# Layer 1 attention, first steps: the eighth tile's score matmuls moved to steps 0 and 1, and three other moves

## The chip, the cores and the metric

The kernel runs as one program on 1 core of one Trainium2 chip. The metric is the device time of one execution in microseconds (us); lower is better. Engines are named as the profile names them: PE (TensorE matmuls) and PEld (its weight loads), DVE (VectorE), ACT (ScalarE), POOL (GpSimd), SP (SyncE, which starts the plain DMAs). Each engine works its own list of instructions in order and waits on semaphores that the others raise.

## The reference, cut to what matters

Two layers on 4 x 1024 rows of 256 numbers. Layer 0 is a causal cross attention and a mixture of eight experts. The change lies where layer 0's experts end and layer 1's attention begins:

```
x = x + L0_ffn(layernorm(x))                    # top-2 of 8 experts per row
# layer 1: 16 heads of width 16 over 77 keys, no mask
q = layernorm(x) as (rows, 16 heads, 16), then @ Wq
energy = q . k ;  attention = softmax(energy / 16)
x = x + (attention @ v) @ Wo.T + bo
x = x + L1_ffn(layernorm(x))                    # gelu, low rank
```

## The kernel before, in words

`experts_and_attend` writes out one list per engine by hand. The first part of each list is the expert part: 32 full steps of 256 row slots (`step(t)`), each with an up and a down product, whose results ACT copies out (`y`) and SP stores to DRAM. The last ones run together with the preparation of layer 1's first row tiles. The second part is a loop over `k in STEPS` (0 to 32).

Layer 1 works on 32 tiles of 128 rows, `f` = 0 to 31. To make a tile ready takes:

1. `gather(f)` on POOL: two indirect DMAs fetch the rows' two expert results. The first 8 tiles use stores that are done earlier; from `f == 8` on `gather` waits for the last store of the expert part.
2. `rows_in_full(f)` on DVE: weigh and add them, then mean and variance (last instruction: `ve_a`, L2001).
3. `deviation(f)` on POOL: the power -1/2 (L1415) and the shift (L1418).
4. `normed_rows(f)` on ACT (L1848), `rows_transposed(f)` on PE (L1713), `high(f)` on ACT (L1842) and `low(f)` on DVE: the normalised rows, transposed, as two float16 parts.
5. `scores(f, i)` on PE (L1644), i = 0 to 3, each followed by `maximum(f, i)` on DVE (L2010): the energies of a tile, a quarter at a time, of which only the row maximum is kept. All quarters of the later tiles share one PSUM bank, so quarter i + 1 waits for the maximum of quarter i. `maxima(g)` and `maxima_transposed(g)` then prepare the maxima of four tiles.

Eight tiles (`AHEAD`, `SOON_ROWS = 8`) go through 1 to 4 during the expert part, and seven of them (`EARLY`) through 5. The eighth tile (number 7) has its scores in step k = 2.

A group of four tiles (512 rows) has four steps, one for four heads each. Step k does `scores_by_key(k)` on PE (L1673, energies with keys on partitions, ending with a fourth term that subtracts the maxima), two `exps(k, half)` on ACT (L1854, softmax's exponentials), and, for the step before, `values(k-1)` on PE (L1685) and `values_out(k-1)` on ACT (L1860). Beside it, it takes tile f = k + 5 through 5, tile k + 6 through 4 and tile k + 7 through 2. From k = 5 on it also finishes tile k - 5 (heads, projection, residual). PE's step begins with `scores(k + 5, 0)`, which waits for `high(k + 5)`. In steps 0 to 4 PE also runs `awake(4)` up to three times (L1719): products into an unused bank whose result nobody reads.

On ACT a step is `normed_rows(f + 1)`, `exps(k, 0)`, (heads,) `values_out(k - 1)`, `exps(k, 1)`, `high(f + 1)`. On POOL an iteration for tile f is `gather(f + 2)`, `deviation(f)`, `biased(f - 8)` (L1424). The exponentials need another function table on ACT than the experts' gelu. L1819, behind the last copy of `y`, runs one exponential of a 128 x 1 tile (`early_a`), so that the table is loaded there.

Of the kernel before, what the change touches and what calls it, by code (L numbers as in the profile page):

```python
# [31 lines left out]
P = 128  # L32
# [1254 lines left out]
def experts_and_attend(nc, A, G):  # L1287
# [3 lines left out]
    with ExitStack() as ctx:  # L1291
# [38 lines left out]
        rec = Q.sb("rec_a", [P, 2, HEADS])  # L1330
        o = Q.sb("o_a", [P, 2, D])
        oT = Q.sb("oT_a", [P, 2, D])
        early = Q.sb("early_a", [P, 1])
        banks = ctx.enter_context(nc.psum_tensor("banks_ea", [P, 8, 512], F32))
        up_ps, xT_ps, y_ps = [banks[:, i, :] for i in range(4)], banks[:, 4, :], [banks[:, i, :] for i in (5, 6)]
        sT_ps, pr_bank, v_ps, s_ps, t_bank = banks[:, 0:4, :], banks[:, 4, :], banks[:, 5, :], banks[:, 6, :], banks[:, 7, :]
# [34 lines left out]
        with nc.Block() as block:  # L1371

            @block.gpsimd
            def _(pool):
# [72 lines left out]
                pool.wait_ge(k1_ok, KN)  # L1447
                pool.wait_ge(bo_in, 16)
                for f in range(SOON_ROWS, NT):
                    if f + 2 < NT:  # L1450
                        gather(f + 2)
                    deviation(f)
                    if f >= LAG:
                        biased(f - LAG)
                for f in range(NT - LAG, NT):
# [38 lines left out]
            def _(pe):  # L1494
# [161 lines left out]
                def scores_by_key(k):  # L1656
                    g, c, i = k // 4, k % 4 // 2, k % 2
                    b, slot = g // 2, g % 3
                    pe.wait_ge(lo_ok, 4 * g + 4)
                    after(pe, exp_ok, 2 * k)  # L1660
                    for term in range(4):
                        if term == 3:
                            pe.wait_ge(mT_ok, g + 1)
                            if tile(k + 5) and k + 5 not in EARLY:
                                scores(k + 5, 1)
                        for r in range(4):
                            rows, head = slice(32 * r, 32 * r + 32), 8 * c + 2 * r + i
                            keys = ds(head * KEYS, KEYS)
                            w, v = ((G["khi"][1][rows, b, keys], xhi[slot][rows, c, :]),
                                    (G["khi"][1][rows, b, keys], xlo[slot][rows, c, :]),  # L1670
                                    (G["klo1"][rows, b, keys], xhi[slot][rows, c, :]),
                                    (mrows[rows, 2 * c + i, :], mT[rows, g % 2, :]))[term]
                            last = mm(sT_ps[0:KEYS, r, :], w, v, start=term == 0, stop=term == 3)  # L1673
                            if term == 3 and r % 2:
                                last.then_inc(sT_done, 1)
# [40 lines left out]
                def awake(count):  # L1716

                    for i in range(count):
                        mm(pr_ps, G["ident16"][:, :], G["khi"][1][:, 0, 0:D], start=True, stop=True)  # L1719
# [18 lines left out]
                for k in STEPS:  # L1738
                    f, n = k + 5, k - 5
                    filled = 0 <= k < 5  # L1740
                    if tile(n):
                        heads_out(n, k)
                    late = tile(f) and f not in EARLY
                    if late:
                        scores(f, 0)
                    if 0 <= k < QUARTERS:
                        scores_by_key(k)
                    if filled:
                        if k == 4:
                            pe.wait_ge(mT_ok, 2)  # L1750
                        awake(4)
                    if tile(n):
                        heads_transposed(n)
                    if 0 <= k - 1 < QUARTERS:
                        values(k - 1)
                    if late:
                        scores(f, 2)
                    if filled:
                        awake(4)
                    if tile(n):  # L1760
                        projection(n)
                    if tile(f + 1) and f + 1 not in AHEAD:
                        rows_transposed(f + 1)
                    if filled:
                        awake(4)
                    if late:
                        scores(f, 3)
                    if (k + 1) % 4 == 0 and 0 <= (k + 1) // 4 < GROUPS:
                        maxima_transposed((k + 1) // 4)
# [11 lines left out]
            def _(act):  # L1781
# [11 lines left out]
                def step(t):  # L1793
                    for q in range(QS):
                        act.wait_ge(up_done, FIRST_Q + QS * t + q + 1)
                        if isinstance(t, int) and t == 0 and q < 2:
                            act.wait_ge(turned, 2 * (SH - 1) + q + 1)
                        else:
                            act.wait_ge(hlo_ok, FIRST_Q + QS * t + q - 1)
                        nc.scalar.activation(h[:, q % 2, :], up_ps[q], ACT.Gelu, scale=1 / WSCALE).then_inc(gelu_ok, 1)  # L1800
                        if isinstance(t, int) and t == 0 and q == 1:
                            short_result(SH - 1)
                    f = t - TURNED if isinstance(t, int) else -1
                    if f in AHEAD:
                        normed_rows(f)
                    if not isinstance(t, int) or t + 1 < FULL:
                        rows(SH + t + 1)
                    if f in AHEAD:
                        high(f)
                    if isinstance(t, int) and t + 1 == FULL:  # L1810
                        maxima(0)
                    act.wait_ge(down_done, FIRST_DOWN + QS * t + QS)
                    act.wait_ge(y_out, stored(t))
                    if isinstance(t, int) and t == 0:
                        act.wait_ge(odd_out, 16 * (SH // 2))
                    for n in range(2):
                        nc.scalar.activation(y[:, n, :], y_ps[n][:, 0:D], ACT.Copy, scale=1 / WSCALE).then_inc(y_ok, 1)  # L1817
                    if isinstance(t, int) and t + 1 == FULL:
                        nc.scalar.activation(early[:, :], G["neghalf"][:, :], ACT.Exp)  # L1819

                def short_result(s):
                    act.wait_ge(down_done, s + 1)
# [62 lines left out]
                for k in STEPS:  # L1885
                    f, n = k + 5, k - 5
                    ahead = not tile(f + 1) or f + 1 in AHEAD
                    if not ahead:
                        normed_rows(f + 1)
                    if 0 <= k < QUARTERS:  # L1890
                        exps(k, 0)
                    if tile(n):
                        heads(n)
                    if 0 <= k - 1 < QUARTERS:
                        values_out(k - 1)
                    if 0 <= k < QUARTERS:
                        exps(k, 1)
                    if not ahead:
                        high(f + 1)
                    if (k + 1) % 4 == 0 and 0 <= (k + 1) // 4 < GROUPS:  # L1900
                        maxima((k + 1) // 4)
# [8 lines left out]
            def _(dve):  # L1910
# [156 lines left out]
                for k in STEPS:  # L2067
# [2 lines left out]
                        low(f)  # L2070
                    if tile(n):
                        sums(n)
                    late = tile(f) and f not in EARLY
                    if late:
                        maximum(f, 0)
                    if tile(n):
# [345 lines left out]
```

## Time and profile before

| | us |
|---|---|
| median of 3 runs (995.8 to 999.16) | 997.5 |
| profiled execution, its own time | 1003.9 |
| span in the profile of that execution | 1001.9 |
| PE busy (92% of the span) | 918.6 |
| DVE busy (62%) | 616.3 |
| ACT busy (51%) | 513.4 |
| POOL busy (42%) | 422.1 |

The profiled execution took 6.4 us more than the median of the runs. All times of the trace count from the start of its span. The last expert step's matmuls end near 719.7 us, step k = 0 starts at 719.75, the last exponential of layer 1 at 887.7, and the feed-forward part follows from 903. The trace gives for each instruction its start, its duration and, in brackets, how long the engine was idle before it and who ended that.

### The profile page before, as it was taken

The numbers are of one execution on the slowest core, as the hardware profiler recorded it, in microseconds if no ns is written. First come the engines' busy times: TensorE is split into PE (matmuls) and PEld (weight loads), VectorE is DVE, ScalarE is ACT, GpSimd is POOL, SyncE is SP. The second block draws the span as 40 slices with busy tenths as digits, with TensorE's granted clock in tenths as the row PEclk, the third lists the DMA queues.
The fourth block names the chain that finished last, engine by engine and source line by source line (L and its number), as shares of the span: only waits on it lengthen the run. The fifth ranks groups of instructions, "written<-read, shape, count | busy, mean of one in ns | idle before, by whom it ended". The sixth has DMA issues, their size and how long they took to land. (4 is left out here: it accounts for less than half of the span.)

```text
span 1001.9 us, 23945 instructions
## 1 busy us (share of the span) xinstructions
PE 918.6 (92%) x8022; PEld 640.7 (64%) x8022; DVE 616.3 (62%) x1517; ACT 513.4 (51%) x873; POOL 422.1 (42%) x573
## 2 busy tenths in 40 slices
PE   6799999997458999999999999999989999889995
PEld 4555656554226788898898888888734444454552
DVE  3577888885787434454554545677468888545661
ACT  1478888886352433333333333333456767645663
POOL 2387777772201122334333224553176665204450
PEclk9999999999876999999999999999989999999998
DMA  6423444424541112111111212232143221000112
GB/s 178 89 65 106 114 145 117 141 88 151 154 160 43 44 44 59 43 43 54 54 43 48 60 44 67 90 90 68 33 113 91 81 78 39 2 1 15 51 46 61
DMA packets 73731, 75.46 MB, mean 75 GB/s; under 512 B 22730, under 2 KB 66874, under 8 KB 73626
## 3 DMA queue, kind: packets, MB, share of 16 engines
q1 hardware_dynamic: 67146, 56.31, 18.8%
q0 software_dynamic: 6480, 17.70, 6.7%
q8 instruction: 72, 1.18, 0.5%
q14 instruction: 33, 0.27, 0.1%
HBM read 51.64 MB, written 22.34 MB: 74 GB/s over the span
## 5 line engine op out<-in xcount | busy, mean ns | idle before, releaser
L1925 DVE CAST hh_e<-h_e 128x512 f16<-128x512 f32 x128 | 57.7, 451 | 151.6 <-ACT h_e L1800 87.7
L1564 PE MATMUL banks_ea<-xT_e,experts 128*128 128x256 f16 x512 | 139.6, 273 | 0.0
L1579 PE MATMUL banks_ea<-experts,hh_e 128*128 x512 | 139.6, 273 | 0.0
L1566 PE MATMUL banks_ea<-xT_e,experts 128*128 128x256 f16 x512 | 139.6, 273 | 0.0
L1580 PE MATMUL banks_ea<-experts,hh_e 128*128 x512 | 139.6, 273 | 0.0
L1565 PE MATMUL banks_ea<-xT_e,experts 128*128 128x256 f16 x512 | 139.6, 273 | 0.0
L1578 PE MATMUL banks_ea<-experts,hh_e 128*128 x512 | 139.6, 273 | 0.0
L1800 ACT ACTIVATE h_e<-banks_ea 128x512 f32<-128x512 f32 x128 | 76.4, 597 | 87.3 <-PE banks_ea L1566 87.3
L1383 POOL DMA_INDIRECT x_e<-xh_scratch,token x33 | 36.8, 1114 | 151.5 <-PE banks_ea L1505 105.5
L1927 DVE TENSOR_TENSOR hh_e<-h_e,hh_e 128x512 f16<-128x512 f32 x128 | 88.6, 692 | 4.4
L1854 ACT ACTIVATE experts<-banks_ea 77x1024 f32<-77x1024 f32 x64 | 64.8, 1014 | 41.0 <-PE banks_ea L1673 41.0
L625 POOL TENSOR_TENSOR experts<-keys,blocks 128x616 f16<-128x616 f16 x64 | 76.5, 1216 | 0.0
L1408 POOL DMA_INDIRECT w_late<-y_scratch,slots_t x64 | 62.5, 977 | 30.7 <-issue 16.7
L2010 DVE TENSOR_REDUCE lx<-banks_ea 128x4 f32<-128x308 f32 x128 | 60.3, 471 | 18.5 <-PE banks_ea L1644 18.0
L835 ACT ACTIVATE experts<-sT_ps 77x1024 f32<-77x1024 f32 x64 | 65.1, 1016 | 7.3 <-PE sT_ps L694 4.2
L1790 ACT ACTIVATE xT_e<-banks_ea 128x512 f16<-128x512 f32 (+1 forms) x39 | 21.8, 558 | 91.3 <-PE banks_ea L1505 91.3
L1380 POOL COPY idx_e<-token 128x2 int32 x19 | 11.6, 611 | 119.1 <-PE banks_ea L1505 119.1
L2327 ACT ACTIVATE experts<-h_ps_f,experts 128x512 f32<-128x512 f32 x64 | 43.2, 688 | 30.2 <-PE h_ps_f L2269 30.2
L928 DVE TENSOR_REDUCE qcat<-s_ps 128x8 f16<-128x616 f32 x64 | 51.0, 798 | 8.5 <-PE s_ps L720 4.3
L1817 ACT ACTIVATE y_e<-banks_ea 128x256 f32<-128x256 f32 x64 | 21.1, 381 | 67.0 <-PE banks_ea L1580 67.0
L1579 PEld LDWEIGHTS banks_ea<-experts,hh_e 128*128 128x128 f16 x512 | 50.0, 98 | 6.2
L1565 PEld LDWEIGHTS banks_ea<-xT_e,experts 128*128 x512 | 50.0, 98 | 6.2
(376 smaller groups left out, 2193.8 us busy)
## 6 DMA issues: line engine op xcount, KB each, us to landing
experts<-in_L_ffn_w SPq DMA_DIRECT2D x22, 512.0 KB, 4.0
y_scratch<-y_e SPq DMA_DIRECT2D x32, 256.0 KB, 3.3
x<-in_x SPq DMA_DIRECT2D x32, 128.0 KB, 3.2
experts<-in_x SPq DMA_DIRECT2D x64, 64.0 KB, 2.4
x_scratch<-x SPq DMA_DIRECT2D x16, 256.0 KB, 2.5
xh_scratch<-xn SPq DMA_DIRECT2D x16, 256.0 KB, 2.7
w_late<-in_L_ffn_w SPq DMA_DIRECT2D x8, 512.0 KB, 4.6
w_late<-x_scratch SPq DMA_DIRECT2D x32, 128.0 KB, 2.6
```

Of the source, the lines that this page charges most:

```text
L625: nc.gpsimd.tensor_tensor(bd[:, f % 2, flat(i, 2), :, :], G["khi"][0][:, b, heads].rearrange("p (q k) -> p q k", q=2)[:, :, None, :] .broa ...
L835: nc.scalar.activation(prob[:, k % 2, qh, :, :], sT_ps[0:KEYS, :, :], ACT.Exp).then_inc(exp_ok, 1)
L1408: pool.indirect_dma_start(out=rows[:, f % 4, :], out_offset=None, in_=A["y"][0:EARLY_ROWS, :] if f < TB else A["y"], in_offset=bass.Indire ...
L1564: mm(out, w[0], xT[0][:, c, :], start=c == 0, stop=False)
L1565: mm(out, w[0], xT[1][:, c, :], start=False, stop=False)
L1566: last = mm(out, w[1], xT[0][:, c, :], start=False, stop=c == DC - 1)
L1578: mm(out, a[0], w[0], start=m == 0, stop=False)
L1579: mm(out, a[0], w[1], start=False, stop=False)
L1580: last = mm(out, a[1], w[0], start=False, stop=m == 7)
L1800: nc.scalar.activation(h[:, q % 2, :], up_ps[q], ACT.Gelu, scale=1 / WSCALE).then_inc(gelu_ok, 1)
L1854: nc.scalar.activation(prob[:, k % 2, 2 * half:2 * half + 2, :], sT_ps[0:KEYS, 2 * half:2 * half + 2, :], ACT.Exp, scale=1.0 / 16).then_in ...
L1927: nc.vector.tensor_tensor(hh[1][own], h[own], hh[0][own], ALU.subtract).then_inc(hlo_ok, 1)
```

## The change

Four moves, no work added or removed:

- **Scores.** Tile 7's four `scores` leave step 2. Quarters 0 and 1 go to step 0 and quarters 2 and 3 to step 1, one ahead of and one behind the first `awake(4)`. DVE's four `maximum` go with them, to the head of DVE's steps 0 and 1, ahead of `rows_in_full(8)`.
- **Deviations.** On POOL, from tile 8 on, `deviation(f)` stands ahead of `gather(f + 2)` and not behind it.
- **Normalisation.** On ACT, in steps 2 to 4, `normed_rows(f + 1)` stands behind `exps(k, 0)` and not ahead of it.
- **Table.** The small exponential that loads the table stands behind `maxima(0)`, ahead of the last two copies of `y`. Its output tile is taken from another place in memory.

```diff
-        early = Q.sb("early_a", [P, 1])
+        early = L.sb("early_a", [P, 1])
...
                 for f in range(SOON_ROWS, NT):
+                    deviation(f)
                     if f + 2 < NT:
                         gather(f + 2)
-                    deviation(f)
...
-                            if tile(k + 5) and k + 5 not in EARLY:
+                            if tile(k + 5) and k + 5 not in AHEAD:
                                 scores(k + 5, 1)
...
-                    late = tile(f) and f not in EARLY
+                    late = tile(f) and f not in AHEAD
...
                         scores_by_key(k)
+                    if k < 2:
+                        scores(SOON_ROWS - 1, 2 * k)
                     if filled:
...
                         awake(4)
+                    if k < 2:
+                        scores(SOON_ROWS - 1, 2 * k + 1)
...
                         maxima(0)
+                        nc.scalar.activation(early[:, :], G["neghalf"][:, :], ACT.Exp)
                     act.wait_ge(down_done, FIRST_DOWN + QS * t + QS)
...
-                    if isinstance(t, int) and t + 1 == FULL:
-                        nc.scalar.activation(early[:, :], G["neghalf"][:, :], ACT.Exp)
...
-                    if not ahead:
+                    if not ahead and k >= 5:
                         normed_rows(f + 1)
                     if 0 <= k < QUARTERS:
                         exps(k, 0)
+                    if not ahead and k < 5:
+                        normed_rows(f + 1)
...
-                    late = tile(f) and f not in EARLY
+                    late = tile(f) and f not in AHEAD
+                    if k < 2:
+                        maximum(SOON_ROWS - 1, 2 * k)
+                        maximum(SOON_ROWS - 1, 2 * k + 1)
```

The order of instructions, at three places. In the names, banks_ea is PSUM; x_e holds the transposed maxima, kc the normalised rows, experts is memory lent to this stage (the exponentials among others), and w_late holds both the fetched rows and the first transposed ones.

PE, steps 0 to 1, from behind the four terms of step 0; - is before, + is the change:

```order
-L1719 MATMUL banks_ea<-keys,ident 128x256 x12
+L1644 MATMUL banks_ea<-keys,w_late 128x308
+L1719 MATMUL banks_ea<-keys,ident 128x256 x4
+L1644 MATMUL banks_ea<-keys,w_late 128x308
+L1719 MATMUL banks_ea<-keys,ident 128x256 x8
```

Two quarters of tile 7's scores now stand among the twelve filling matmuls of step 0; step 1 takes the other two, and step 2 has none.

ACT, step 2, from the second exponential of step 1; before:

```order
L1854 ACTIVATE experts<-banks_ea 77x1024
L1848 ACTIVATE kc<-experts,shift_a,rstd_a 128x256
L1854 ACTIVATE experts<-banks_ea 77x1024
L1860 ACTIVATE experts<-banks_ea 128x512
L1854 ACTIVATE experts<-banks_ea 77x1024
L1842 ACTIVATE experts<-banks_ea 128x2x128
```

and now (L1857 is the exponential, L1851 the normalisation, L1863 the values, L1845 the transposed rows):

```order
L1857 ACTIVATE experts<-banks_ea 77x1024 x2
L1851 ACTIVATE kc<-experts,shift_a,rstd_a 128x256
L1863 ACTIVATE experts<-banks_ea 128x512
L1857 ACTIVATE experts<-banks_ea 77x1024
L1845 ACTIVATE experts<-banks_ea 128x2x128
```

The normalisation of tile 8 changed places with the first exponential of step 2; the values, the second exponential and the transposed rows still follow it.

POOL, from the gathers of tiles 8 and 9; before:

```order
L1408 DMA w_late<-y_scratch,slots_t 128x256 x6
L1415 TENSOR_TENSOR rstd_a<-ve_a,neghalf 128x1
L1418 TENSOR_SCALAR shift_a<-mv_a,rstd_a 128x1
L1424 TENSOR_TENSOR X_soon<-X_soon,bo_a 128x256
L1408 DMA w_late<-y_scratch,slots_t 128x256 x2
```

and now:

```order
L1408 DMA w_late<-y_scratch,slots_t 128x256 x4
L1415 TENSOR_TENSOR rstd_a<-ve_a,neghalf 128x1
L1418 TENSOR_SCALAR shift_a<-mv_a,rstd_a 128x1
L1408 DMA w_late<-y_scratch,slots_t 128x256 x2
L1424 TENSOR_TENSOR X_soon<-X_soon,bo_a 128x256
```

Before, the six indirect DMAs of tiles 8, 9 and 10 stood ahead of tile 8's deviation; now the four of tiles 8 and 9 do, and tile 10's two stand behind it.

## Rows read from the trace of the kernel before

**Rows 1.** Who waited for whom on ACT, 715 to 745 us (total, times, longest).

```profile
ACT kc L1848 <- POOL shift_a L1418: 4.8, 2, 3.8
```

**Rows 2.** Timeline of PE: starts of steps 0, 2, 3, 4, 5, 7 and 8.

```profile
719.75 0.41 PE L1673 MATMUL banks_ea<-w_late,keys 32*77 32x512 f16 x4
...
728.29 0.42 PE L1673 MATMUL banks_ea<-w_late,keys 32*77 32x512 f16 x4 [0.60 <-ACT experts L1854]
...
735.21 0.30 PE L1644 MATMUL banks_ea<-keys,experts 128*128 128x308 f16 x1 [1.56 <-ACT experts L1842]
...
743.00 0.42 PE L1644 MATMUL banks_ea<-keys,experts 128*128 128x308 f16 x1 [0.23 <-DVE lx L2010]
...
748.61 0.29 PE L1644 MATMUL banks_ea<-keys,experts 128*128 128x308 f16 x1 [0.22 <-DVE lx L2010]
...
758.95 0.29 PE L1644 MATMUL banks_ea<-keys,w_late 128*128 128x308 f16 x1 [0.23 <-DVE lx L2010]
...
764.51 0.29 PE L1644 MATMUL banks_ea<-keys,w_late 128*128 128x308 f16 x1
```

**Rows 3.** Timeline of ACT: end of the expert part, and step 2.

```profile
717.29 0.59 ACT L1875 ACTIVATE x_e<-banks_ea 128x512 f16<-128x512 f16 x1
719.85 0.66 ACT L1817 ACTIVATE y_e<-banks_ea 128x256 f32<-128x256 f32 x2 [1.97 <-PE banks_ea L1580]
720.53 1.28 ACT L1819 ACT_TABLE_LOAD   x1
...
721.93 1.91 ACT L1854 ACTIVATE experts<-banks_ea 77x1024 f32<-77x1024 f32 x2
...
731.99 0.60 ACT L1848 ACTIVATE kc<-experts,shift_a,rstd_a 128x256 f32<-128x256 f32 x1 [3.84 <-POOL shift_a L1418]
732.49 1.00 ACT L1854 ACTIVATE experts<-banks_ea 77x1024 f32<-77x1024 f32 x1
733.40 0.58 ACT L1860 ACTIVATE experts<-banks_ea 128x512 f32<-128x512 f32 x1
733.87 1.01 ACT L1854 ACTIVATE experts<-banks_ea 77x1024 f32<-77x1024 f32 x1
734.78 0.38 ACT L1842 ACTIVATE experts<-banks_ea 128x256 f16<-128x256 f32 x1
```

**Rows 4.** Timeline of POOL: gathers (L1408) and deviations from tile 8 on.

```profile
723.45 1.04 POOL L1408 DMA_INDIRECT w_late<-y_scratch,slots_t  x1 [14.04 <-DMA y_scratch<-y_e]
...
729.80 0.95 POOL L1408 DMA_INDIRECT w_late<-y_scratch,slots_t  x1 [0.30 <-issue]
730.76 0.83 POOL L1415 TENSOR_TENSOR rstd_a<-ve_a,neghalf 128x1 f32<-128x1 f32 x1
731.69 0.27 POOL L1418 TENSOR_SCALAR shift_a<-mv_a,rstd_a 128x1 f32<-128x1 f32 x1
...
735.10 0.58 POOL L1415 TENSOR_TENSOR rstd_a<-ve_a,neghalf 128x1 f32<-128x1 f32 x1
```

**Rows 5.** Timeline of DVE: tile 8's sum and variance, tile 10's sum.

```profile
727.55 0.48 DVE L1991 SCALAR_TENSOR_TENSOR wp<-w_late,cw_t 128x256 f32<-128x256 f32 x1 [6.38 <-DMA w_late<-y_scratch,slots_t]
...
729.27 0.15 DVE L2001 TENSOR_SCALAR ve_a<-mv_a 128x1 f32<-128x1 f32 x1
...
736.96 0.48 DVE L1991 SCALAR_TENSOR_TENSOR wp<-w_late,cw_t 128x256 f32<-128x256 f32 x1
```

**Rows 6.** PE by windows of 1 us: length, busy (count), granted clock, DMA share, GB/s.

```profile
723.00:724.00 1.00, 0.01 (x4) 1.00 0.00 0
...
734.00:735.00 1.00, 0.00 (x0) 1.00 0.42 111
...
737.00:738.00 1.00, 1.00 (x8) 0.50 0.06 16
...
743.00:744.00 1.00, 1.00 (x9) 0.61 0.21 78
```

**Rows 7.** The line view of L1408, all 64 gathers: issue to landing.

```profile
DMA to landing us min/median/max: 2.7/3.1/3.9
```

## The prediction

> **What bounds the kernel now.** I read the waits of the stretch first, then followed the longest one through the timelines of ACT, POOL, DVE and PE, and last looked at TensorE's clock. The chain that ended last is of no use here: it reaches back only into the feed-forward part.
>
> From step 4 on the loop is even. Steps 5 and 6 together take 758.95 - 748.61 = 10.34 us, 5.17 each, and step 7, which also prepares the maxima of four tiles, takes 764.51 - 758.95 = 5.56 [rows 2]. PE waits only 0.2 us at each of those starts. Steps 2 and 3 stand out: step 3 begins at 735.21 and step 4 at 743.00, so step 3 takes 7.79.
>
> Who holds step 3 back? PE idled 1.56 us in front of it for ACT's L1842, the transposed rows of tile 8 [rows 2]. On ACT these end a run of five instructions that began with tile 8's normalisation at 731.99; for that ACT idled 3.84 us, waiting for POOL's shift [rows 1, 3]. The exponentials of step 2 stood behind it. On POOL the deviation began at 730.76, at the very end of an indirect DMA issue (729.80 + 0.95 = 730.75) [rows 4]; its input, the variance, was ready at 729.27 + 0.15 = 729.42 [rows 5]. So the deviation stood 1.3 us in a queue behind tile 10's gather, which nobody needed yet: DVE took that at 736.96 [rows 5].
>
> The second thing to see is the clock. Between 734 and 735 us PE did nothing at all; by 737 its granted clock had gone from 1.00 to 0.50, the lower level of 1.2 GHz, and it came back to 2.4 GHz within 743 to 744 (mean 0.61) [rows 6]. In between PE was busy without a pause, so step 3 was long because PE was slow. An idle microsecond alone doesn't bring this: 723 to 724 was as empty and the clock stayed at 1.00 [rows 6].
>
> **The change part by part.** The profiled execution took 1003.9 us, 6.4 above the median of 997.5; I work out the sum against its trace and take it off both.
>
> *Deviation ahead of gather, normalisation behind exponential.* These go together. The start of the chain stays: tile 8's gather begins at 723.45 when the last `y` is stored, and DVE takes its data at 727.55 [rows 4, 5]. The variance is then ready at 729.42. Now POOL has only tile 8's and 9's four issues ahead of the deviation. Six end at 730.75, and from the first to the sixth issue are five pitches, (729.80 - 723.45) / 5 = 1.27 each, so four end near 723.45 + 3 x 1.27 + 0.95 = 728.2 and POOL is waiting. The deviation starts at 729.5, 1.25 sooner than 730.76. From its start to the normalisation's took 731.99 - 730.76 = 1.23, so the normalisation starts at 730.75. This row's power took 0.83 us, the next one 0.58 [rows 4]; with the short one it is 730.5.
>
> From the normalisation to the transposed rows took 734.78 - 731.99 = 2.79. The first exponential, 733.40 - 732.49 = 0.91 of it, now goes ahead [rows 3]. It has time to: PE began step 2's energies at 728.29, and even with a microsecond for its four terms the exponential can run from about 729.4 to 730.4, before the normalisation can start. So 2.79 - 0.91 = 1.88 is left, and the transposed rows come at 730.75 + 1.88 = 732.6, or 732.4 with the short power, against 734.78. That is **2.2 to 2.4 sooner; I take 2.3**. Step 3 starts at 735.21 - 2.3 = 732.9.
>
> *The clock.* PE ends step 2 with tile 8's transposition and some filling, which follow the normalisation and so come 1.25 sooner; step 3 comes 2.3 sooner; the empty stretch of 1.56 between them shrinks by about 1. The waits inside step 2 go too, because no score has to wait for a maximum there. I expect no fall of the clock. Step 3 also prepares the maxima of four tiles, as step 7 does, but finishes no older tile; at full clock I give it 5.3, between 5.17 and 5.56. It took 7.79, and step 4 took 748.61 - 743.00 = 5.61 against 5.17. The fall cost (7.79 - 5.3) + (5.61 - 5.17) = 2.9; ends 2.7 and 3.1, or zero if it stays. I take **2.9**, because the cause I see for it is removed.
>
> *Scores.* Four matmuls and four maxima move and none are added. In step 0 they stand where PE filled its wait for the exponentials. In step 1 the last quarter must wait for the maximum of the third, about 0.4 us, in front of `values(0)`; this delays the values and the second exponential of step 1. Covered: the chain above waits for tile 8's variance until 729.42. On DVE the maxima run while it idles 6.38 us for the gather [rows 5]. If that cover were gone, each would cost 0.5. In the sum: nothing by themselves.
>
> *Table.* `maxima(0)` ends at 717.29 + 0.59 = 717.88 and the copy of `y` starts at 719.85, bound by PE; the load with the small exponential takes 721.93 - 720.53 = 1.40 [rows 3]. It fits, with 0.57 to spare. The first exponentials come about 1.1 sooner, and step 1 with them. This gain ends at step 2, where tile 8's data, not PE, decides; I count nothing. The Trainium skill, "ScalarE: Activation LUTs", What ACT_TABLE_LOAD costs, speaks against this part: it adds a drain to the load and puts each switch at about 2.66 us, by which the copies of `y`, and everything from tile 8's gather on, would come about 0.8 late and the sum would be -4.4. The trace does not agree: the load began 0.02 after the copies ended (719.85 + 0.66 = 720.51) and took 1.28 [rows 3].
>
> *Behind the moved deviation.* Tile 10's gather starts after tile 8's deviation instead of at about 728.5, so near 730.8. From a gather's first issue to DVE's use took 727.55 - 723.45 = 4.1 [rows 4, 5], so it is there at 734.9. DVE wanted it 736.96 - 735.21 = 1.75 after step 3's start; now that is 734.65. It comes some 0.25 late, in front of a maximum that PE does not need at once; between 0 and 0.3, taken as zero. After that the order closes a loop: deviation, gather two tiles on, sum, deviation. It takes 4.1 + 1.87 (727.55 to 729.42) + about 1.4 for power and shift with their waits = 7.4 us for two tiles, against 10.34 for two steps. SP's loads hang on DVE's sums and only move forward.
>
> *Sum:* -2.3 - 2.9 = -5.2. Later steps and the feed-forward part are bound by PE and take the shift over whole. The profiled execution comes to 998.7 and the median to **992.3**.
>
> **The rivals.**
>
> *Only the queue's part counts.* The clock's fall hung on one particular run of idle and busy time. The three runs lie 3.4 us apart, about what one fall costs, so the median run before may not have had it, or the fall comes elsewhere after the change. Then -2.3: 995.2. For it: as empty a microsecond at 723 left the clock up [rows 6]. Against it: the same program has the same idle times in every run.
>
> *A table switch with a drain.* The cover of 0.57 is thin. If ACT, behind `maxima(0)`, first had to drain for as long as the load itself takes, 1.28, the copies would start at 717.88 + 1.28 + 1.40 = 720.56 and not 719.85, and store, gather and chain 0.7 later: -4.5, 993.0. Against it: no such pause stands ahead of the load at 720.53 [rows 3]. The page of the Trainium skill that is named above describes such a drain.
>
> *A new wait absorbs it.* Tile 10's gather, started 2.3 later, lands later than the pattern, DVE stands at it with two maxima behind, and step 4 waits for PE's last score. At the longest landing in the trace, 3.9 against 3.1 [rows 7], that is 0.8 more, no more than a third of the gain from the queue. To leave nothing it would need a stall of 5; around no change, 997.
>
> *Slower: the closed loop becomes the pitch.* If a gather took over 2.9 us longer than 4.1, two tiles would take over 10.34 and every one of the 22 remaining gathers would pay. To end 3 us slower it must take back 8.2, 0.37 a step, so 3.7 us later landings throughout: 1000.5 or more. The spread of landings, 2.7 to 3.9 [rows 7], speaks against it; the feed-forward weights that are loaded from step 4 on speak a little for it.
>
> **How the numbers follow.** A measurement of this kernel can tell about 0.3%, 3.0 us, from no change; so faster means under 994.5. Forecast 0.52 (its own range 990.5 to 994.0), queue's part alone 0.29, drain 0.04, absorbed 0.10, slower 0.05. Faster by over 0.3%: 0.51 of the forecast, 0.07 of the queue's part (for a fall now and then), 0.03 of the drain: 0.61. Slower by over 0.3%: 0.05. Within: 0.34. The range goes from 990.3, the upper ends of both terms (-2.4 and -3.1) with 1.7 for the runs' own spread, to 996.9, the queue's part alone with the same; what is left out is the slower case, most of the absorbed one and some of the low end.
>
> **What would show it right or wrong.** In the profile after, measured from the start of step 0: the power of tile 8 starts right behind the variance, not behind a DMA issue; ACT's wait for the shift falls from 3.8 us to under 1 and stands behind an exponential; step 3 starts 13.2 us after step 0 (735.21 - 719.75 = 15.46 before) [rows 2], and step 4 some 5.2 later at a granted clock of 1.00; the copy of `y` still waits for PE. I am wrong if the clock still falls in steps 2 to 4, if step 3's start moves by under 1.5 us, or if DVE's sums wait for gathers from step 3 on.

## The result and the profile after

The change made the kernel slower: a median of 1002.3 us in 8 runs (998.7 to 1005.0) against 997.5 in 8 runs of before (995.0 to 999.5), a ratio of 1.0043 [1.0022, 1.0064]. Forecast was 992.3. The profiled execution of after took 1003.1, its span is 1000.8. Lines of `experts_and_attend` are numbered higher after the change: L1991 is now L1996, L1994 is L1999, L2001 is L2006, L1848 is L1851, L1854 is L1857; L1408 to L1424 and L1644 to L1713 kept theirs.

The page, its busy times; before had DVE 616.3 and POOL 422.1, with the same instructions:

```profile
span 1000.8 us, 23944 instructions
...
PE 916.5 (92%) x8022; PEld 637.4 (64%) x8022; DVE 625.8 (63%) x1517; ACT 514.7 (51%) x873; POOL 427.7 (43%) x573
```

DVE is busy 9.5 us longer and POOL 5.6. The numbers of instructions are the same, so some have become longer. Which ones comes further down; first the start of layer 1, which the prediction was about.

The timeline of POOL, gathers and deviations from tile 8 on, which answers to [rows 4]:

```profile
726.05 0.94 POOL L1408 DMA_INDIRECT w_late<-y_scratch,slots_t  x1 [0.30 <-issue]
728.34 0.57 POOL L1415 TENSOR_TENSOR rstd_a<-ve_a,neghalf 128x1 f32<-128x1 f32 x1 [1.34 <-DVE ve_a L2006]
729.00 0.26 POOL L1418 TENSOR_SCALAR shift_a<-mv_a,rstd_a 128x1 f32<-128x1 f32 x1
729.43 1.07 POOL L1408 DMA_INDIRECT w_late<-y_scratch,slots_t  x1 [0.16 <-issue]
```

The deviation of tile 8 waits 1.34 us for its variance, no longer behind a gather, and the gather stands behind it. The timeline of ACT, the table and step 2, which answers to [rows 3]:

```profile
716.65 1.28 ACT L1816 ACT_TABLE_LOAD   x1
717.95 0.20 ACT L1816 ACTIVATE early_a<-neghalf 128x1 f32<-128x1 f32 x1
718.61 0.66 ACT L1822 ACTIVATE y_e<-banks_ea 128x256 f32<-128x256 f32 x2 [0.46 <-PE banks_ea L1580]
...
729.30 0.60 ACT L1851 ACTIVATE kc<-experts,shift_a,rstd_a 128x256 f32<-128x256 f32 x1 [0.65 <-POOL shift_a L1418]
```

The table is loaded in time: the copies of `y` still wait 0.46 us for PE. The wait for tile 8's shift is 0.65 instead of 3.84. The timeline of PE, starts of steps 3, 4 and 6 (step 0 starts at 718.50), which answers to [rows 2]:

```profile
731.61 0.30 PE L1644 MATMUL banks_ea<-keys,experts 128*128 128x308 f16 x1 [0.78 <-ACT experts L1845]
...
737.48 0.29 PE L1644 MATMUL banks_ea<-keys,experts 128*128 128x308 f16 x1 [0.44 <-DVE lx L2015]
...
748.44 0.29 PE L1644 MATMUL banks_ea<-keys,experts 128*128 128x308 f16 x1 [0.23 <-issue]
```

Step 3 starts 731.61 - 718.50 = 13.11 us after step 0 (15.46 before) and step 4 18.98 (23.25 before). PE by windows, which answers to [rows 6], has a granted clock of 1.00 throughout; before it was 0.50 from 737 to 743:

```profile
734.00:737.00 3.00, 2.62 (x24) 1.38 (x16) 2.27 (x7) 2.59 (x5) 2.67 (x4) 1.00 0.37 108
737.00:743.00 6.00, 5.33 (x48) 2.65 (x47) 4.78 (x13) 4.38 (x7) 4.79 (x8) 1.00 0.46 135
```

So at step 4 the profiled execution is 4.3 us ahead. At the last exponential of the loop it is not: that starts 886.71 - 718.50 = 168.21 after step 0, against 167.98 in the profiled execution of before. Some 4.5 us are lost in the steady steps, which the prediction had left alone. It is more, in fact: behind step 25 that execution of before lost another 1.2 us, because its clock fell once more (0.50 from 877 to 880). Against executions of before without these falls the loss is 6.0, as the experiments show.

**Where they are lost.** The line view of three groups, before (behind the bar: busy us, mean ns of one, idle time in front):

```profile
L1991 DVE SCALAR_TENSOR_TENSOR wp<-w_late,cw_t 128x256 f32<-128x256 f32 x32 | 15.2, 475 | 6.4 <-DMA w_late<-y_scratch,slots_t 6.4
L1994 DVE SCALAR_TENSOR_TENSOR experts<-w_late,cw_t,wp 128x256 f32<-128x256 f32 x24 | 11.6, 485 | 0.9
...
L1424 POOL TENSOR_TENSOR experts<-experts,bo_a 128x256 f32<-128x256 f32 x24 | 17.1, 725 | 0.0
```

The same after:

```profile
L1996 DVE SCALAR_TENSOR_TENSOR wp<-w_late,cw_t 128x256 f32<-128x256 f32 x32 | 18.9, 591 | 3.6 <-DMA w_late<-y_scratch,slots_t 3.6
L1999 DVE SCALAR_TENSOR_TENSOR experts<-w_late,cw_t,wp 128x256 f32<-128x256 f32 x24 | 18.3, 762 | 0.8
...
L1424 POOL TENSOR_TENSOR experts<-experts,bo_a 128x256 f32<-128x256 f32 x24 | 20.4, 866 | 0.3
```

The two weighted sums of DVE and POOL's bias add (`biased`) are longer, at the same shapes. The timelines say why. Before, DVE and then POOL, one steady step:

```profile
755.51 0.47 DVE L1991 SCALAR_TENSOR_TENSOR wp<-w_late,cw_t 128x256 f32<-128x256 f32 x1
756.02 0.48 DVE L1994 SCALAR_TENSOR_TENSOR experts<-w_late,cw_t,wp 128x256 f32<-128x256 f32 x1
```

```profile
752.96 0.26 POOL L1418 TENSOR_SCALAR shift_a<-mv_a,rstd_a 128x1 f32<-128x1 f32 x1
753.18 0.73 POOL L1424 TENSOR_TENSOR X_soon<-X_soon,bo_a 128x256 f32<-128x256 f32 x1
754.07 1.03 POOL L1408 DMA_INDIRECT w_late<-y_scratch,slots_t  x1 [0.16 <-issue]
755.41 0.95 POOL L1408 DMA_INDIRECT w_late<-y_scratch,slots_t  x1 [0.30 <-issue]
```

After:

```profile
750.18 0.72 DVE L1996 SCALAR_TENSOR_TENSOR wp<-w_late,cw_t 128x256 f32<-128x256 f32 x1
750.94 0.84 DVE L1999 SCALAR_TENSOR_TENSOR experts<-w_late,cw_t,wp 128x256 f32<-128x256 f32 x1
```

```profile
747.77 0.27 POOL L1418 TENSOR_SCALAR shift_a<-mv_a,rstd_a 128x1 f32<-128x1 f32 x1
748.20 1.03 POOL L1408 DMA_INDIRECT w_late<-y_scratch,slots_t  x1 [0.16 <-issue]
749.53 0.94 POOL L1408 DMA_INDIRECT w_late<-y_scratch,slots_t  x1 [0.30 <-issue]
750.50 0.99 POOL L1424 TENSOR_TENSOR X_soon<-X_soon,bo_a 128x256 f32<-128x256 f32 x1
```

Before, the bias add stood directly behind the deviation and ended at 753.91, 1.6 us ahead of DVE's sums. With the gather moved behind the deviation, two issues (2.27 us, from 748.20 to 750.47) stand between them, and the bias add falls on the sums: 750.50 to 751.49 against 750.18 to 751.78. All three read two tiles of SBUF each, and all three stretch. In before the gather issues ran beside the sums (755.41 to 756.36) and nothing stretched. The rest of after says the same: its 37 sums of layer 1 that lie across a bias add took 0.59 to 0.84 us, 0.76 on average, the other 27 took 0.48.

DVE has little room for it. Busy time by engine, 770 to 830 us, the sum of before and then that of after:

```profile
sum 60.00, PE 57.17 PEld 28.86 DVE 52.90 ACT 41.40 POOL 40.33; mean PE 9.53 PEld 4.81 DVE 8.82 ACT 6.90 POOL 6.72
```

```profile
sum 60.00, PE 55.88 PEld 27.16 DVE 55.05 ACT 40.33 POOL 40.91; mean PE 9.31 PEld 4.53 DVE 9.18 ACT 6.72 POOL 6.82
```

DVE goes from 88% to 92% of this stretch and PE from 95% to 93%. What PE waits for there (us in total, times, longest), before and then after:

```profile
PE banks_ea L1644 <- DVE lx L2010: 1.8, 8, 0.2
```

```profile
PE banks_ea L1644 <- DVE lx L2015: 3.8, 16, 0.3
```

The scores wait for DVE's maxima twice as often. Between the starts of the first sum above and of the next one lie 5.65 us (755.83 - 750.18), against 5.16 before (755.51 - 750.35).

### The profile page after: what moved, and what is told of

It reads as the page before. It is cut to its first block and busy times, and to the rows that moved or that the text cites. A ratio compares the mean times of both kernels' runs of the same rounds, so it can differ in the third digit from the quotient of the medians.

```text
span 1000.8 us, 23944 instructions
## 1 busy us (share of the span) xinstructions
PE 916.5 (92%) x8022; PEld 637.4 (64%) x8022; DVE 625.8 (63%) x1517; ACT 514.7 (51%) x873; POOL 427.7 (43%) x573
## 5 line engine op out<-in xcount | busy, mean ns | idle before, releaser
L1857 ACT ACTIVATE experts<-banks_ea 77x1024 f32<-77x1024 f32 x64 | 64.8, 1014 | 41.8 <-PE banks_ea L1673 41.8
L1408 POOL DMA_INDIRECT w_late<-y_scratch,slots_t x64 | 63.1, 986 | 31.1 <-issue 17.1
```

Source lines behind the costliest of these rows:

```text
L1408: pool.indirect_dma_start(out=rows[:, f % 4, :], out_offset=None, in_=A["y"][0:EARLY_ROWS, :] if f < TB else A["y"], in_offset=bass.Indire ...
L1857: nc.scalar.activation(prob[:, k % 2, 2 * half:2 * half + 2, :], sT_ps[0:KEYS, 2 * half:2 * half + 2, :], ACT.Exp, scale=1.0 / 16).then_in ...
```

## The experiments

The measure I use below comes from each kernel's one profile: from the start of step 0 to the start of step 4, and to the start of the loop's last exponential. It leaves out what happens ahead of the loop and behind it. Times are medians, ratios are against runs of before on the same chip in the same job; a ratio is worked out from all the runs, so it need not be that of the two medians.

| kernel | step 3 | step 4 | last exponential | sums, mean ns | clock in steps 3, 4 |
|---|---|---|---|---|---|
| before, profiled first | 15.46 | 23.25 | 167.98 | 475, 485 | falls |
| before_again | 15.43 | 23.26 | 166.75 | | falls |
| before_c | 15.48 | 23.37 | 166.78 | | falls |
| before_b | 15.43 | 20.74 | 163.95 | | 1.00 |
| before_d | 15.47 | 20.78 | 164.03 | | 1.00 |
| after | 13.11 | 18.98 | 168.21 | 591, 762 | 1.00 |
| pool_alone | 14.57 | 19.87 | 169.16 | 591, 762 | 1.00 |
| bias_late | 15.49 | 23.33 | 172.59 | 579, 737 | falls |
| bias_first | 13.16 | 20.18 | 164.87 | 476, 499 | falls for 3.4 us |
| pool_undone | 14.32 | 19.84 | 163.05 | 491, 485 | 1.00 |
| bias_one_input | 13.15 | 18.81 | 161.79 | 504, 506 | 1.00 |
| pool_early | 13.11 | 20.93 | 168.26 | 487, 499 | falls |
| pool_early_lag | 13.13 | 20.52 | 163.77 | 477, 485 | 1.00 |
| hybrid | 13.51 | 18.88 | 162.13 | 477, 485 | 1.00 |

Two questions: is it the bias add beside the sums that costs the steady steps, or something else that the new order of POOL's queue does (the gathers above all)? And what of the predicted gain was there to be had?

**bias_late: the suspected cost alone, put into the kernel before.** Gather and deviation stay in the old order; only the bias add goes where it meets DVE's sums.

```diff
                     if f + 2 < NT:
                         gather(f + 2)
+                    if f > LAG:
+                        biased(f - LAG - 1)
                     deviation(f)
-                    if f >= LAG:
-                        biased(f - LAG)
-                for f in range(NT - LAG, NT):
+                for f in range(NT - LAG - 1, NT):
```

> The kernel before with the bias add alone moved: on POOL gather, bias add of the tile before, deviation. The gather still stands ahead of the deviation. Theory A: the bias add now runs while POOL would wait for the variance, that is while DVE sums; the sums take about 0.72 and 0.84 us, steps 5 to 24 take 5.6 instead of 5.2 to 5.3, and the time rises by 6 to 10 us to 1003 to 1007. Theory B: as before, 996 to 999.

Measured: 1003.0 against 998.4, 1.0061 [1.0036, 1.0086]. The line view has the stretched rows of after, and the gathers are as they were before:

```profile
L1991 DVE SCALAR_TENSOR_TENSOR wp<-w_late,cw_t 128x256 f32<-128x256 f32 x32 | 18.5, 579 | 6.4 <-DMA w_late<-y_scratch,slots_t 6.4
L1994 DVE SCALAR_TENSOR_TENSOR experts<-w_late,cw_t,wp 128x256 f32<-128x256 f32 x24 | 17.7, 737 | 0.8
```

Its clock falls in steps 3 and 4, so it is to be held against the executions of before that also fall: 172.59 - 166.77 = 5.8 us in the loop. From step 4 to the last exponential it takes 149.26, after took 149.23 and before_c 143.41. The bias add's place is enough to produce the loss.

**bias_first and pool_undone: the change without it.** bias_first puts the bias add ahead of the gather and keeps all else; pool_undone has the old order on POOL.

```diff
                     deviation(f)
-                    if f + 2 < NT:
-                        gather(f + 2)
                     if f >= LAG:
                         biased(f - LAG)
+                    if f + 2 < NT:
+                        gather(f + 2)
```

> The change with one more swap: on POOL the bias add stands right behind the deviation, as before, and the gather behind both (deviation, bias add, gather). Theory A, POOL's bias add and DVE's two weighted sums (two inputs each) slow each other when they run at the same time: the sums return from 0.72 and 0.84 us to 0.48 each, the bias add from 0.98 to 0.73, a step from 5.6 to 5.2 (5.4 on the mean of four), and the start-up gain is kept: 993 to 996 us. Theory B, it is the gather behind the deviation (its loop, or its descriptors) that lengthens the steps: sums and steps stay as in the change, 1000 to 1004 us.

```diff
-                    deviation(f)
                     if f + 2 < NT:
                         gather(f + 2)
+                    deviation(f)
                     if f >= LAG:
                         biased(f - LAG)
```

> The change with POOL's order of before; scores, normalisation and table stay moved. Theory A and B both: the sums are 0.48, the steps 5.2 to 5.4. By my prediction's chain the deviation of tile 8 again waits for tile 10's gather (1.25 us), and only the exponential that goes ahead of the normalisation is left of the start-up gain, about 1 us: 996 to 997. If the scores or the table are worth something by themselves, step 3 starts over 2 us sooner after step 0 than before and the time is under 995.5.

Measured: bias_first 999.2, 0.9995 [0.9972, 1.0018]; pool_undone 995.9, 0.9977 [0.9953, 1.0002]. In both the sums are short again, and the steady steps are back: 143.2 us from step 4 to the last exponential in pool_undone, 144.7 in bias_first, against 149.2 in after and 143.2 in before_b. So it is not the gather behind the deviation (theory B), which bias_first has in every step. But bias_first missed its 993 to 996. It starts step 3 as early as after does, and then DVE waited 1.91 us for tile 10's gather (0.75 in after), step 4 came 1.2 later than in after, and the clock fell from 738.8 to 742.2. The gather now stands behind a bias add too, of 0.7 us; that this is the cause isn't shown, since pool_early, below, waits as long without it. A late gather is what I had in mind with the wait that absorbs the gain; here it takes 1.2 of the 2.3 us.

**pool_alone: the new order on POOL, nothing else of the change.**

```diff
                 for f in range(SOON_ROWS, NT):
+                    deviation(f)
                     if f + 2 < NT:
                         gather(f + 2)
-                    deviation(f)
```

> The kernel before with POOL's order of the change alone. By my chain the deviation of tile 8 starts 1.25 us sooner but the first exponential still stands behind the normalisation: step 3 starts 14.1 to 14.3 us after step 0 (15.46 before, 13.1 in the change). By the theory of the slowed sums, steps 5 to 24 take 5.5 to 5.7 and the last exponential starts 168 to 172 after step 0. If the slow sums needed one of the other three moves, they are 0.48 here.

One run, 1004.4. The sums take 591 and 762 ns as in after. Step 3 starts 0.9 sooner than before, so of the 2.35 us that the change gains there the POOL part brings 0.9 by itself (14.57, where 14.1 to 14.3 was expected); pool_undone, the other three parts without it, brings 1.1. The two together bring 0.3 more than the sum of both. From step 4 to the last exponential it takes 149.29: the slow sums need none of the other three moves.

**bias_one_input: the same place and order, but a POOL instruction with one input.** The bias add becomes a product with 1.0; the bias of the output projection is left out of the result, and the POOL instruction is of another kind.

```diff
-nc.gpsimd.tensor_tensor(X(f), X(f), bo[:, :], ALU.add).then_inc(xb_ok, 1)
+nc.gpsimd.tensor_scalar(X(f), X(f), 1.0, None, ALU.mult).then_inc(xb_ok, 1)
```

> The change with POOL's bias add replaced by a multiplication by 1.0 of the same 128 x 256 numbers, one input instead of two; this leaves the bias of layer 1's output projection out. If DVE's sums are slowed by any reading of SBUF by POOL beside them, they stay above 0.6 us; if it takes POOL's second input, they return to 0.48 and a step to 5.2 to 5.4.

One run, 995.3. The POOL instruction lies across the sums as in after, timelines of POOL and DVE:

```profile
753.86 1.02 POOL L1424 TENSOR_SCALAR X_soon<-X_soon 128x256 f32<-128x256 f32 x1
```

```profile
753.69 0.48 DVE L1996 SCALAR_TENSOR_TENSOR wp<-w_late,cw_t 128x256 f32<-128x256 f32 x1
754.20 0.50 DVE L1999 SCALAR_TENSOR_TENSOR experts<-w_late,cw_t,wp 128x256 f32<-128x256 f32 x1
```

The sums keep 0.48 to 0.50 here and 504 and 506 ns on average, and the loop is 161.79, the shortest of all. Not every step is so clean; the next one:

```profile
759.08 0.89 POOL L1424 TENSOR_SCALAR const<-const 128x256 f32<-128x256 f32 x1
```

```profile
759.12 0.66 DVE L1996 SCALAR_TENSOR_TENSOR wp<-w_late,cw_t 128x256 f32<-128x256 f32 x1
759.82 0.48 DVE L1999 SCALAR_TENSOR_TENSOR experts<-w_late,cw_t,wp 128x256 f32<-128x256 f32 x1
```

Single sums reach 0.68, and POOL's instruction, 0.88 with no sum beside it, reaches 1.03. So something of the collision is left, but most is gone: being beside POOL's work is not by itself what costs 0.3 us a step. The bias add has a second tile to read and this one has not; it is also another operation, of 0.88 us alone and not 0.73. Which of the two counts is not shown, because no other two-input instruction of POOL was tried.

**pool_early, pool_early_lag, hybrid: keeping the gain without the cost.** pool_early has the new order for the first two tiles alone; pool_early_lag and hybrid also start the bias adds two tiles later (`LAG` 10), so that none stands in the queue of the first gathers; hybrid has bias_first's order. The diff is that of pool_early_lag.

```diff
-                KN, LAG = 2 * B * DC, 8
+                KN, LAG = 2 * B * DC, 10
...
-                    deviation(f)
+                    if f < SOON_ROWS + 2:
+                        deviation(f)
                     if f + 2 < NT:
                         gather(f + 2)
+                    if f >= SOON_ROWS + 2:
+                        deviation(f)
```

> The change with POOL's new order for tiles 8 and 9 alone; from tile 10 on gather, deviation, bias add as before. If the loss is the bias add running beside DVE's sums, it is gone from step 5 on (sums 0.48, steps 5.17 to 5.43) and the start-up stays as early as in the change (step 3 starts 13.1 us after step 0, step 4 at 19.0): about 1 us better than the change with POOL's old order, 994 to 996. If the deviation ahead of the gather is worth nothing, it ends level with that one.

> As pool_early, and each bias add two tiles later (10 behind and not 8), so that POOL has none between the deviations and gathers of tiles 8 and 9. If POOL's queue still holds back the sums of tiles 10 and 11, step 4 starts some 0.5 us sooner than in pool_early: 993.5 to 995.5. If not, the same as pool_early.

> The change with the bias add in front of the gather and two tiles later (10 behind): tiles 8 and 9 have deviation, gather; from tile 10 on deviation, bias add, gather. Both parts of the theory together: step 3 starts 13.1 us after step 0 and no sum is slowed, so the last exponential starts 162 to 164 us after step 0 and the time is 993.5 to 996. If the gathers behind the deviations cost something by themselves, it is above 996.

Measured: pool_early 997.3, 0.9999 [0.9977, 1.0020] (one of its 12 runs took 1794.1 us and is not in the ratio); pool_early_lag 995.4, 0.9981 [0.9960, 1.0002]; hybrid 996.4, 0.9980 [0.9959, 1.0001]. hybrid's loop is 162.13 with step 4 at 18.88: the gain at the start is kept (1.9 us against before_b) and the sums stay at 477 and 485 ns. Its 996.4 lies just above the 996 that I had set for a cost of the gathers themselves, but from step 4 to the last exponential it takes 143.25, as long as before_b (143.21), so there is no such cost. Its ratio is 0.2% below 1, its median 0.06% below that of before (997.0), and its interval, like pool_undone's and pool_early_lag's, just takes in no change. None of these can be called faster; hybrid is the best by the trace among those that compute everything, because what it saves can be pointed at.

In pool_early and pool_early_lag DVE waited 2.0 and 2.3 us for tile 10's gather, though POOL's order up to its issue is that of after. Why it came later there I can't say.

**pu_no_scores and pu_no_table: pool_undone without one of the small parts.** One puts the eighth tile's scores back into step 2, the other the small exponential back behind the copies of `y`.

> The change with POOL's old order and tile 7's scores back in step 2; normalisation and table stay moved. My prediction gave the scores nothing by themselves: step 3 again 14.3 us after step 0. If they are worth something, the fourth term of step 2 waits for a maximum again, the exponential that goes ahead of the normalisation is late, and step 3 starts at 14.8 to 15.5.

> The change with POOL's old order and the table loaded behind the copies of y again; normalisation and scores stay moved. My prediction gave the table nothing by itself: step 1 starts 4.2 us after step 0 instead of 3.2, step 3 still at 14.3. If it matters, step 3 comes later.

One run each, 997.0 and 995.2. Step 3 starts at 14.59 without the scores' move and 14.32 without the table's, against 14.32 in pool_undone: the scores bring 0.27 us, the table nothing. With the scores in step 2 PE waited 1.92 us for a maximum, and nearly all of that was hidden behind tile 8's chain. With the table loaded late, step 1 starts 4.24 after step 0 instead of 3.17, and the microsecond is gone by step 3, as the prediction said.

**before_again, before_b, before_c, before_d and filled: does the clock fall in every run of before?** The first four are the kernel before, unchanged; filled adds filling matmuls at the end of step 2, where PE idled.

> The kernel before, unchanged, for what its runs share: 995 to 999.5 us. If the fall of the clock in steps 3 and 4 belongs to every run, its profile shows it again (granted clock 0.50 for some 6 us behind the gap ahead of step 3) and step 3 takes 7 to 8 us; if it belongs to the one profiled run of 1003.9 us, step 3 takes about 5.3 and the profiled run is some 3 us shorter.

> The kernel before, unchanged. Theory C: a timed run of about 996 us is one in which the clock did not fall in steps 3 and 4 (step 3 takes 5.3, the last exponential starts about 164.1 us after step 0), one of about 1002 is one in which it did (7.8 and 166.7). Then the fall that I priced at 2.9 is missing in the median run. Theory D: every run has the fall, and the two kinds differ elsewhere; then 7.8 and 166.7 in a run near 996 too.

> The same kernel once more, for a run of the other kind. Theory C and D as for before_b.

> The same kernel once more, for a run of the other kind. Theory C and D as for before_b.

```diff
+                    if k == 2:
+                        awake(12)
```

> The kernel before with 12 more filling matmuls (1.3 us) at the end of PE's step 2, in the gap of 1.56 us ahead of step 3; their result is not read and PE waits there anyway. If that gap decides whether the clock falls in steps 3 and 4, the runs of 1002 us at a mean clock of 0.968 go, the rest stays at 994 to 998, and the profile shows 1.00 in steps 3 and 4 with step 3 taking about 5.3 instead of 7.8. If the two kinds of run come from other places, they stay as they are.

The four profiled executions took 1002.4 (falls), 995.7 (doesn't), 1002.3 (falls) and 997.5 (doesn't). PE by windows, 735 to 745 us, in before_b and then in before_c:

```profile
735.00:745.00 10.00, 9.34 (x87) 4.63 (x85) 7.51 (x21) 6.89 (x12) 7.33 (x11) 1.00 0.61 145
```

```profile
735.00:745.00 10.00, 9.76 (x64) 4.11 (x64) 5.60 (x14) 5.28 (x8) 5.82 (x8) 0.66 0.22 68
```

The two come out of the same 1.56 us idle stretch in front of step 3. One kernel thus has executions of two kinds, with and without this fall. It costs 166.77 - 163.99 = 2.8 us in the loop (means of the two pairs); the other 3.8 of the 6.6 between the spans of before_b and before_c (993.7 and 1000.3) lie elsewhere, in stretches where before_c's clock is also lower: 0.91 against 1.00 at 240 to 260 us, 0.66 against 0.72 from there to 320, 0.97 against 1.00 at 870 to 890. before_again was also timed: its 12 runs (994.8 to 1003.1, ratio 1.0003 [0.9976, 1.0030]) split into four of 994.8 to 996.5 at a mean clock of 0.976 to 0.978 and eight of 1000.3 to 1003.1 at 0.968 to 0.972. Their median is 1001.2, against 998.4 for the 35 other runs of before: a dozen runs of one kernel can lie that far off, so the loss of after rests on its trace and on bias_late more than on its median. It also stands at the highest mean clocks: after's three runs at 0.978 and 0.979 took 998.7 to 1001.5, the 17 runs of before at 0.976 to 0.980 beside before_again 994.2 to 998.5. filled took 997.5, 0.9996 [0.9975, 1.0017]: its profile has no fall in steps 3 and 4, but neither have two of five of before, so one profile does not show that the filling did it. Runs with a lower clock remain (down to 0.969, 1002.0), so filling that one gap did not settle the kernel's other stretches.

## Why the prediction was wrong

**The step that failed: "Later steps and the feed-forward part are bound by PE and take the shift over whole."** They lost 6.0 us: from step 4 to the last exponential it is 149.23 after against 143.21 in before_b. In these steps PE's 0.2 us waits at every start were for DVE's maxima, and DVE was 88% busy (770 to 830 us). The prediction read them as PE's bound and asked only of the gather, the instruction that the deviation was moved past, when it would land. It did not follow the instruction behind both. `biased` stood right behind the deviation and was pushed back two issues, 2.3 us, onto DVE's sums. Its price is in the traces: the sums grew by 0.12 and 0.28 us each (591 - 475 and 762 - 485 ns), 3.7 + 6.7 = 10.4 in all, of which 6.0 show.

The Trainium skill, "SBUF — State Buffer", Who interferes with whom, states the rule that I passed over: a DVE instruction with two SBUF inputs contends with a GpSimd instruction that reads SBUF. The traces agree that these two collide. That section of the Trainium skill calls the port pair that they share an exclusive lock; here neither engine is simply held until the other is done, all three instructions run longer (0.48 to 0.72 and 0.84, and 0.73 to 0.99). The sum is close to taking turns all the same: one after the other they need 0.48 + 0.48 + 0.73 = 1.69 us, side by side they took 1.60 (750.18 to 751.78). The one-input instruction of bias_one_input reads SBUF too, and beside it the sums of all tiles came to only 504 and 506 ns on average (475 and 485 in before).

**The side and the rivals.** The slower side had a chance of 0.05 and one mechanism, gathers that land late in every step. In after DVE waited for three gathers in all, 3.6 us together against 6.4 before, and for none from tile 11 on. The sign came by another way, which was not among the rivals. Nor did the signs of being wrong look for it: the clock kept 1.00 in steps 2 to 4, step 3 moved by 2.35, and one sum, tile 10's, waited 0.75 for its gather from step 3 on. All three look at the start of the loop, and the loss came behind it.

**The clock, -2.9: the size was right, its place in the sum wrong.** A fall costs 2.8. But the term was taken from a profiled execution of 1003.9 us and subtracted from a median of 997.5. The eight runs of before beside the change all lie under 999.5; the profiled executions of before with the fall took 1002.3 to 1003.9, those without it 995.7 and 997.5. So the median most likely had no fall to lose, and the term should have been 0 there. The text saw the 6.4 us and named the possibility, at 0.29. Its argument against it, "the same program has the same idle times in every run", holds for the idle time in front of step 3 (1.56 or 1.57 in all five) and yet decides nothing: three of the five fall and two do not.

**The queue and the normalisation, -2.3: right.** 15.46 became 13.11, 2.35 sooner. By step 4 some of it was spent: 18.98 against 20.76 without a fall (before_b, before_d), 1.8, with 0.75 us of waiting for tile 10's gather, forecast at 0 to 0.3.

**Scores and table, 0: right.** 0.27 and 0.0. No drain showed: the load took 1.28 us and the exponential began 0.02 behind it, so the rival by that mechanism is out. The 2.66 us that the Trainium skill, "ScalarE: Activation LUTs", What ACT_TABLE_LOAD costs, gives for a switch did not show here either.

**The sum by what was measured:** -1.8 at step 4, 0 for the clock, +6.0 in the steady steps: +4.2, so 997.5 + 4.2 = 1001.7 against 1002.3 measured. Behind the last exponential nothing changed: 1000.8 - 886.71 = 114.1 us in after, 993.7 - 879.60 = 114.1 in before_b.

## What to carry to other kernels

When one instruction is moved ahead of another in an engine's queue, write down when each instruction behind the pair now runs, in a steady step, and what the other engines do at that time: here the pair that was looked at gained 2.35 us once, and the one behind it lost 0.3 us in each of some twenty steps. An engine that is 88% busy and ends each short wait of PE is the bound as much as PE is. And before a term is taken from one profiled execution, see how that execution stands to the median: what it has and the median has not can't be gained.

## What was not expected of the hardware

- The collision shows as mutual stretching: two sums of 0.48 us and a bias add of 0.73 took 0.72, 0.84 and 0.99 when they overlapped. Gather issues on POOL beside the same sums stretched nothing.
- The same program, with the same idle stretch of 1.56 us on PE, kept its clock in two of five profiled executions and fell to 0.50 for some 6 us in three. Which runs fall, and what in the program would decide it, stays open.
- A gather's landing varied more than [rows 7] showed, up to 4.3 us in after and 4.9 in pool_early_lag, with the same issues; why stays open.
